# A sparse-attention block on one core: two shared PSUM banks, a new order of its stages, and shorter square roots

## The chip, the core and the metric

The kernel runs on one core of one Trainium2 chip. Its engines are TensorE (PE, with its weight loads PEld), VectorE (DVE), ScalarE (ACT), GpSimd (POOL) and SyncE (SP), which issues the DMAs. Each takes its own instructions in the order in which they stand in the program, and they meet at semaphores. The metric is device time in microseconds, less is better.

## The reference, cut to what matters

The input is x of shape [16, 512, 128]: 16 batches of 512 tokens.

```
...
q, k, v = heads(x @ w_q.T), heads(x @ w_k.T), heads(x @ w_v.T)      # 16 heads of 8
q, k = q * rsqrt(mean(q*q) + 1.19e-7), k * rsqrt(mean(k*k) + 1.19e-7)
s = tanh((q k^T / sqrt(8)) / 50) * 50, causal                       # 512 x 512 per head
x = layernorm(x + (softmax(s) v) @ w_o.T)
w = x @ router_w + router_b;  the 63 tokens of the largest w are selected
h = rmsnorm(x_sel, ln1); q, k = rope(h wq), rope(h wk); v = h wv    # 63 x 63 attention, 16 heads
x1 = x_sel + (softmax(q k^T / sqrt(8) + mask) v) @ wo
x2 = x1 + gelu(rmsnorm(x1, ln2) @ w1) @ w2
x = layernorm(x + (x2 * w at the selected tokens, x elsewhere))
...
```

## The kernel before, in words

The batches go in eight pairs. The dense attention is one batch (`/0` or `/1`) at a time, in eight groups of two heads. For each group PE computes scores in two halves (`scores`, L1116, 3 and 5 matmuls) into `ps_s`, ACT applies tanh to each half (L655) and one exp to the group (L667), POOL zeroes what is not causal (L562, four instructions), and every second group PE multiplies by v (`pv`, L1130, 32 matmuls) into `ps_y`.

Around it stand stages, each cut into uses of PE and steps of DVE:

- `prep` (a batch): transpose x, q, k and v, their norm, and the split of q and k into two f16 parts; the low parts are made by POOL (`prep.lo`, L577).
- `fin` (a batch): normalise y (`yU`, `y0`, `y1`, `yT`), project (`wo`), add x (`res`), layernorm: `fin.ln` (moments, L836 to L844), `fin.root1`, `fin.root2`, `fin.x1` (L863).
- `route` (a batch): w is reduced by DVE (`route.w`, L871) from a product made by POOL (`route.xw`), spread and transposed (`row`), and tokens are ranked with `ge` (L887), `eq` (L894) and `rank`.
- `sel` (a pair): gather, rmsnorm, q, k, v with rope, and `R`: the mask's selected rows (L1220, 16 matmuls).
- `att` (a pair): scores `S0`, `S1`, softmax, `P0`, `P1` (transposes), `PV`, `oT`, `wo`, `x1f`, rmsnorm (`ss`, roots, `hn`), `h2T` (L1297), `w1`, gelu in which POOL makes `hh` and `hu`, and ACT a tanh (`g`).
- `late` (a pair): `w2`, scatter (`sc0`, `sc1`), `z0`, `z1`, layernorm (`late.norm`, L1060), store.

**What sets the order.** The body for pair p is 16 steps of two half-steps. In each PE first issues half of the next group's scores and then what `PE_ORDER` lists; DVE and POOL follow `VE_ORDER` and `POOL_ORDER`. `att.P0@-2` is use P0 of stage att for pair p-2, `prep.qk0/0@1` is for batch 0 of pair p+1. The tables don't say when something runs: an engine goes on to its next entry when that entry's semaphores allow. Pairs 3 to 6 run in a hardware loop, the others are written out. After the last scores three more bodies drain `sel`, `att` and `late`.

**PSUM.** `prep` has bank `ps_a`. All other short uses share bank `ps_m`. A use may be written when the one before it has been read: `BANK_READ` lists, by use, the DVE steps to wait for, as `"sel.R": ["sel.vv1@0"]`.

**Roots.** 1/sqrt is a guess from the bits and three Newton rounds of three instructions: with the variance 11 dependent instructions, in two parts. `a & b` in `VE_ORDER` makes two roots in turn, instruction by instruction; six of the seven roots of a pair of batches are made so (`fin/1 & att`, `prep/0 & sel`, `fin/0 & late`), and `prep/1` stands alone.

```
def step(make, name, after=None):            # each step waits for the one before it in its stage
    ...
for step, name, buf, *_ in problems:         # problems: one or two roots
    step(lambda: nc.vector.tensor_tensor(buf[:, 2], buf[:, 1], buf[:, 1], ALU.mult), f"{name}_a{i}")
for step, name, buf, *_ in problems:
    step(lambda: nc.vector.scalar_tensor_tensor(buf[:, 2], buf[:, 2], -0.5, buf[:, 0], ALU.mult, ALU.mult), f"{name}_b{i}")
for step, name, buf, *_ in problems:
    step(lambda: nc.vector.scalar_tensor_tensor(buf[:, 1], buf[:, 2], 1.5, buf[:, 1], ALU.add, ALU.mult), f"{name}_c{i}")
```

## Time and profile before

| | |
|---|---|
| median of 3 runs | 953.69 us (952.84 to 954.15) |
| the profiled execution | 953.16 us, span of its instructions 951.4 us |
| busy: PE, DVE, ACT, POOL | 731.0, 678.2, 609.6, 407.3 us |
| chain that ended last, shares | PE 46%, DVE 29%, issue 13%, ACT 7%, POOL 2% |
| granted TensorE clock, mean | 0.795 of full |

A row of the page names the line, the engine, the operation, output and inputs, a count, the busy time with the mean of one, and the idle time of the engine in front of it with what ended it. A wait row names the waiting engine and line, and whom it waited for. The chain of waits follows the execution back from its end. "issue" is time for which the profile shows no reason. Times in a timeline count from the span's start.

### The profile page before, as it was taken

Reading aid. Unit: us, or ns where it says so; the run is one execution under the profiler, and the core shown is the slowest. Engines: PE = TensorE matmul, PEld = TensorE weight load, DVE = VectorE, ACT = ScalarE, POOL = GpSimd, SP = SyncE. Lnnn points to the kernel's source line nnn. Section 1 sums busy time; section 2 is a strip of 40 time slices with the busy share of each in tenths; the row PEclk is TensorE's granted clock in tenths of the full one; section 3 lists DMA queues with packets and bytes.
Section 4 is the critical chain, followed back from the end, with each engine's and each line's share of the span. In section 5 each row is a group of like instructions: output and inputs, shape, how many; then the busy total and the mean of one; then the engine's idle time right before and its main releaser. Section 6 shows DMA issues by size and latency. Waiting matters only on the chain.

```text
span 951.4 us, 15701 instructions
## 1 busy us (share of the span) xinstructions
PE 731.0 (77%) x4976; PEld 398.3 (42%) x4976; DVE 678.2 (71%) x2013; ACT 609.6 (64%) x403; POOL 407.3 (43%) x776
## 2 busy tenths in 40 slices
...
DMA packets 96898, 36.40 MB, mean 38 GB/s; under 512 B 68018, under 2 KB 94146, under 8 KB 96834
## 3 DMA queue, kind: packets, MB, share of 16 engines
q1 hardware_dynamic: 96834, 35.67, 16.2%
q8 instruction: 25, 0.41, 0.2%
q14 instruction: 39, 0.32, 0.1%
...
## 4 chain that ended last, share of the span: by engine, by line
PE 46%; DVE 29%; issue 13%; ACT 7%; POOL 2%; DVEq 1%; DMA 1%; POOLq 0%; SPq 0%; ACTq 0%
PE ps_y L1130 10%; PE ps_s L1116 9%; PE ps_m L1220 5%; ACT pr L667 4%; PE ps_m L1137 4%; DVE junk L887 3%; ACT th L655 2%; PE ps_a L1168 2%; PE ps_a L1161 2%; PE ps_m L1319 2%; PE ps_m L1187 2%; PE ps_m L1205 2%; PE ps_m L1266 2%; PE ps_m L1280 2%; PE ps_m L1303 1%
## 5 line engine op out<-in xcount | busy, mean ns | idle before, releaser
L655 ACT ACTIVATE th<-ps_s 128x1024 f32<-128x1024 f32 (+1 forms) x256 | 308.8, 1236 | 155.3 <-PE ps_s L1116 149.8
L667 ACT ACTIVATE pr<-th 128x2560 f32<-128x2560 f32 x128 | 298.8, 2335 | 31.0 <-PE ps_y L1130 31.0
L1116 PE MATMUL ps_s<-q_st,k_st 32*128 32x128 f16 (+3 forms) x1024 | 209.8, 342 | 26.2 <-ACT th L655 22.0
L562 POOL TENSOR_SCALAR_AFFINE_SELECT pr<-pr 128x256 f32<-128x256 f32 (+2 forms) x512 | 194.7, 413 | 0.0
L1130 PE MATMUL ps_y<-pr,v_aug 128*32 128x512 f32 (+3 forms) x2048 | 178.2, 496 | 3.8 <-POOL pr L562 3.8
L1116 PEld LDWEIGHTS ps_s<-q_st,k_st 32*128 32x128 f16 x1024 | 84.6, 102 | 125.0 <-issue 60.5
L577 POOL TENSOR_TENSOR st<-qk,st 128x1024 f16<-128x1024 f32 x32 | 73.1, 2303 | 103.7 <-DVE st L803 103.7
L1130 PEld LDWEIGHTS ps_y<-pr,v_aug 128*32 128x32 f32 x2048 | 65.3, 121 | 114.2 <-issue 96.2
L620 POOL TENSOR_TENSOR pool_mark<-head_of 128x1 f32<-128x1 f32 x128 | 26.5, 207 | 187.5 <-ACT pr L667 187.3
L565 POOL TENSOR_TENSOR st<-qk 128x1024 f32<-128x1024 f32 x16 | 30.3, 1893 | 48.9 <-DVE qk L776 48.9
L887 DVE TENSOR_SCALAR_CACHE_REDUCE junk<-w_wide,x 128x512 f32<-128x512 f32 x64 | 47.7, 746 | 2.0
L1220 PE MATMUL ps_m<-masks,E 128*64 128x512 f32 x128 | 43.0, 834 | 7.6 <-DVE vv L960 7.6
L1161 PE MATMUL ps_a<-wT,xT 128*128 128x256 f32 x128 | 41.8, 455 | 8.9 <-DVE qk L776 7.9
L565 POOL TENSOR_TENSOR r<-x,rw_row 128x512 f32<-128x512 f32 x16 | 18.9, 1178 | 58.6 <-DVE x L863 58.6
L1297 PE MATMUL ps_m<-ident,hn 128*128 128x128 f32 x8 | 3.8, 472 | 51.3 <-DVE hn L1017 51.3
L641 ACT ACTIVATE hq<-hu 128x512 f32<-128x512 f32 x8 | 5.0, 630 | 56.9 <-POOL hu L565 56.9
L813 DVE COPY y_u<-ps_y 128x512 f32<-128x512 f32 x32 | 21.9, 684 | 25.3 <-PE ps_y L1130 25.2
L565 POOL TENSOR_TENSOR k_wide<-qkT,head_of 128x1024 f32<-128x1024 f32 x16 | 30.1, 1904 | 19.0 <-DVE qkT L966 19.0
L894 DVE SCALAR_TENSOR_TENSOR junk<-w_wide,x,later 128x512 f32<-128x512 f32 (+1 forms) x64 | 36.0, 562 | 2.0
L637 ACT ACTIVATE pm<-pm 128x1008 f32<-128x1008 f32 x8 | 8.4, 1044 | 42.3 <-DVE pm L979 42.3
L776 DVE COPY qk<-ps_a 128x512 f32<-128x512 f32 x32 | 22.0, 686 | 18.1 <-PE ps_a L1161 18.1
L882 DVE COPY w_wide<-ps_m 128x512 f32<-128x512 f32 x16 | 11.1, 691 | 32.1 <-PE ps_m L1137 24.7
...
## 6 DMA issues: line engine op xcount, KB each, us to landing
...
q_st<-st SPq DMA_TRANSPOSE x16, 4.5
k_st<-st SPq DMA_TRANSPOSE x16, 4.8
...
```

The costliest lines, as they stand in the source:

```text
L562: return nc.gpsimd.affine_select(out=buf, in_=buf, compare_op=ALU.is_ge, fill=0.0, base=0, pattern=[[0, n], [1, P]] if n > 1 else [[1, P]] ...
L565: mul = lambda out, a, b: nc.gpsimd.tensor_tensor(out, a, b, ALU.mult)
L577: pl["prep"].done(nc.gpsimd.tensor_tensor(lo_parts[s], qk_twice[s], hi_parts[s], ALU.subtract), f"lo_{part}", b)
L655: nc.scalar.activation(th[:, gi % 2, c0:c1], ps_s[:, c0:c1], ACT.Tanh, scale=1.0 / (QK_SCALE ** 2 * DH ** 0.5 * SOFTCAP))\
L667: nc.scalar.activation(pr[:, gi % 4, :], th[:, gi % 2, :], ACT.Exp, scale=SOFTCAP)\
L887: step(lambda: nc.vector.tensor_scalar(junk[:, :], w_wide[:, :], x1[:, k, c, D:D + 1], 0.0, ALU.is_ge, ALU.add, accum_out=cnt_ge[:, c:c + ...
L894: step(lambda: nc.vector.scalar_tensor_tensor(junk[:, 0:n], w_wide[:, P * c:], x1[:, k, c, D:D + 1], later[:, 0:n], ALU.is_equal, ALU.mult ...
L1116: last = mm(ps_s[:, c:c + S - P * kb], k_st[32 * j:32 * j + 32, k, kb, g, :], q_st[32 * j:32 * j + 32, k, kb:NT, g, :], start=True, stop=True)
L1130: last = mm(ps_y[32 * j:32 * j + 32, P * kb:S], v_aug[:, k, kb, h, :], pr[:, gi % 4, c:c + S - P * kb], start=(q % 2 == 0 and kb == 0), st ...
L1137: last = tr(ps_m[:, P * c:P * c + P], src(c), ident[:, :])
L1161: last = mm(ps_a[:, 2 * D * (t % 2):2 * D * (t % 2) + 2 * D], xT[:, P * t:P * t + P], wT[:, 0:2, :].rearrange("p a d -> p (a d)"), start=T ...
L1220: last = mm(ps_m[SLOTS * k:SLOTS * k + SLOTS, :], E[:, c, SLOTS * k:SLOTS * k + SLOTS], masks[:, k, c, :], start=(c == 0), stop=(c == NT - 1))
```

## The change

**Banks.** The table `BANK` gives every short use one of the two banks, "a" or "m", `prep` among them, so that a use and the next mostly lie in different banks; `BANK_READ` is new with it. The setup's three matmuls go to `ps_y`.

**Order.** `PE_ORDER`, `VE_ORDER` and `POOL_ORDER` are new; ACT's is as it was.

**Roots.** A polynomial of four instructions takes the place of the three rounds: guess, a, t, then u2, u3, u4, y. The variance is folded into the moments or the reduction in front, but for `prep`, which keeps its own. Eight instructions for `prep`, seven for the others, each root by itself. The moments lose one instruction of six (`sum`), and now four of the five are chained.

```diff
-                for i in (0,) if first else (1, 2):
-                    for step, name, buf, *_ in problems:
-                        step(lambda: nc.vector.tensor_tensor(buf[:, 2], buf[:, 1], buf[:, 1], ALU.mult), f"{name}_a{i}")
...
+                    step(lambda: nc.vector.tensor_scalar(y.bitcast(I32), w.bitcast(I32), -0.5, RSQRT_GUESS, ALU.mult,
+                                                         ALU.add), f"{name}_guess")
+                    step(lambda: nc.vector.tensor_tensor(t, y, y, ALU.mult), f"{name}_a")
+                    step(lambda: nc.vector.tensor_tensor(w, t, w, ALU.mult), f"{name}_t")
+                else:
+                    step(lambda: nc.vector.scalar_tensor_tensor(t, w, q3, w, ALU.add, ALU.mult), f"{name}_u2")
+                    step(lambda: nc.vector.scalar_tensor_tensor(t, t, q2, w, ALU.add, ALU.mult), f"{name}_u3")
+                    step(lambda: nc.vector.scalar_tensor_tensor(t, t, q1, w, ALU.add, ALU.mult), f"{name}_u4")
+                    step(lambda: nc.vector.scalar_tensor_tensor(y, t, q0, y, ALU.add, ALU.mult), f"{name}_y")
...
+BANK = {
...
+    "sel.R": "m",
...
+    "sel.qkv": "a",
+}
...
-    "sel.R": ["sel.vv1@0"],
+    "sel.R": ["prep.xT/1@2", "sel.hnT@0"],
...
-                bank_free("att.h2T", q)
-                pe["att"].done(tr(ps_m[:, 0:P], hn[:, :], ident[:, :]), "h2T", q)
+                bank_free("att.h2T", q)
+                pe["att"].done(tr(at("att.h2T")[:, 0:P], hn[:, :], ident[:, :]), "h2T", q)
...
-                tr(ps_m[:, 0:P], rw_wide, ident[:, :])
+                tr(ps_y[:, 0:P], rw_wide, ident[:, :])
...
+                if q == 0 and isinstance(b.no, int) and b.no == 0:
+                    t_.wait_ge(setup_ve, SETUP_ROUTER)
```

**Place 1: PE, from the projection `wo` of `att` to `h2T`** (the transpose of `hn`), in pair 2's body. Before:

```order
L1292 MATMUL ps_m<-wo,oT 128x128
L1116 MATMUL ps_s<-q_st,k_st 128x256 x2
L1116 MATMUL ps_s<-q_st,k_st 128x384
L1116 MATMUL ps_s<-q_st,k_st 128x128
L1116 MATMUL ps_s<-q_st,k_st 128x512
L1297 MATMUL ps_m<-ident,hn 128x128
```

The change, from right behind `wo`:

```order
L1156 MATMUL ps_s<-q_st,k_st 128x384
L1156 MATMUL ps_s<-q_st,k_st 128x128
L1156 MATMUL ps_s<-q_st,k_st 128x512
L1196 MATMUL ps_m<-ident,x_in 128x128 x4
L1156 MATMUL ps_s<-q_st,k_st 128x256 x2
L1156 MATMUL ps_s<-q_st,k_st 128x384
L1156 MATMUL ps_s<-q_st,k_st 128x128
L1156 MATMUL ps_s<-q_st,k_st 128x512
L1156 MATMUL ps_s<-q_st,k_st 128x384
L1156 MATMUL ps_s<-q_st,k_st 128x128
L1156 MATMUL ps_s<-q_st,k_st 128x512
L1339 MATMUL ps_a<-ident,hn 128x128
```

Between `wo` and `h2T` stand now three halves of scores and the transpose `prep.xT` instead of one half of scores, and `h2T` goes to `ps_a`. Behind `h2T` comes `pv` and then `w1`; before it was `w1` and then `pv`.

**Place 2: DVE, the start of the body.** `cnt_eq` is `eq`, `den` is the softmax's sum, `k_wide<-ps` is a copy of `P0` or `P1`, `qk<-ps` copies q and k. Before:

```order
L894 SCALAR_TENSOR_TENSOR junk,cnt_eq<-w_wide,x,later 128x512
L894 SCALAR_TENSOR_TENSOR junk,cnt_eq<-w_wide,x,later 128x384
L894 SCALAR_TENSOR_TENSOR junk,cnt_eq<-w_wide,x,later 128x256
L894 SCALAR_TENSOR_TENSOR junk,cnt_eq<-w_wide,x,later 128x128
L776 COPY qk<-ps_a 128x2x2x128
L986 TENSOR_REDUCE den<-pm 128x16
L987 RECIPROCAL rden<-den 128x16
L991 COPY k_wide<-ps_m 128x512
L900 TENSOR_TENSOR rank<-cnt_ge,cnt_eq 128x4
L903 TENSOR_SCALAR coef<-cnt_ge 128x4
L907 TENSOR_TENSOR E<-rank,slot_no 128x4x64
L776 COPY qk<-ps_a 128x2x2x128
```

The change:

```order
L923 TENSOR_SCALAR junk,cnt_ge<-w_wide,x 128x512 x4
L810 COPY qk<-ps_a 128x2x2x128
L810 COPY qk<-ps_m 128x2x2x128
L847 COPY y_u<-ps_y 128x512
L1023 TENSOR_REDUCE den<-pm 128x16
L1024 RECIPROCAL rden<-den 128x16
L822 COPY v_aug<-ps_m 128x16x2x8 x2
L854 RECIPROCAL rd<-ps_a 128x32
L856 TENSOR_TENSOR y_tm<-ps_a,rd 128x4x64
L1028 COPY k_wide<-ps_m 128x512
L826 TENSOR_REDUCE qn_v<-st 128x128
L1028 COPY k_wide<-ps_a 128x512
```

The second copy of q and k, for which PE's `prep.v` waits, stands behind one copy and not behind `eq`, `den`, `P0`'s copy and `rank`, which come later; the two copies read different banks.

**Place 3: DVE, from `hn` of `att` to `route.w`** (the reduction of `r`, L871 before and L907 now). Before:

```order
L1017 TENSOR_SCALAR hn<-x1f,sel_v 128x128
L863 TENSOR_SCALAR x<-r,mv,ln_v 128x128 x4
L1020 TENSOR_SCALAR h2T<-ps_m,g 128x128
L1060 TENSOR_SCALAR y_out<-y_out,mv,lo_v 128x128 x8
L1026 COPY hb<-ps_m 128x512
L871 TENSOR_REDUCE x<-r 128x4
```

The change:

```order
L1055 TENSOR_SCALAR hn<-x1f,sel_v 128x128
L783 TENSOR_SCALAR ln_v<-ln_v 128x4
L785 TENSOR_TENSOR ln_v<-ln_v 128x4
L786 TENSOR_TENSOR ln_v<-ln_v 128x4
L788 SCALAR_TENSOR_TENSOR ln_v<-ln_v 128x4
L789 SCALAR_TENSOR_TENSOR ln_v<-ln_v 128x4
L790 SCALAR_TENSOR_TENSOR ln_v<-ln_v 128x4
L791 SCALAR_TENSOR_TENSOR ln_v<-ln_v 128x4
L1058 TENSOR_SCALAR h2T<-ps_a,g 128x128
L899 TENSOR_SCALAR x<-r,mv,ln_v 128x128 x4
L907 TENSOR_REDUCE x<-r 128x4
```

Before, `h2T`, the eight instructions of `late.norm` and a copy stood between `fin.x1` (`x<-r,mv`) and `route.w`, which waits for POOL's product of x1. Now `route.w` stands right behind `fin.x1`, and `late.norm` is behind `g`, ahead of `late.proc`.

## Rows read from the trace of the kernel before

**Rows 1.** The page: busy time of each engine (us, share of the span).

```profile
PE 731.0 (77%) x4976; PEld 398.3 (42%) x4976; DVE 678.2 (71%) x2013; ACT 609.6 (64%) x403; POOL 407.3 (43%) x776
```

**Rows 2.** Windows (us, busy us of PE, PEld, DVE, ACT, POOL, clock): middle, one pair, last pair, tail.

```profile
193.75:713.50 519.75, 435.29 (x3106) 236.90 (x3107) 410.79 (x1208) 378.95 (x251) 249.62 (x470) 0.82 0.18 41
501.90:607.65 105.75, 88.03 (x621) 47.97 (x622) 83.79 (x249) 75.78 (x51) 49.87 (x94) 0.81 0.16 35
713.50:810.60 97.10, 82.12 (x603) 44.12 (x605) 73.37 (x231) 74.72 (x50) 43.23 (x91) 0.83 0.12 27
810.60:951.40 140.80, 77.50 (x395) 48.54 (x395) 81.02 (x294) 18.54 (x13) 23.18 (x32) 0.60 0.04 12
```

**Rows 3.** Waits, 501.9 to 607.65 us (total us, times, longest us).

```profile
ACT th L655 <- PE ps_s L1116: 25.2, 13, 3.9
...
PEld ps_m L1297 <- DVE hn L1017: 8.1, 1, 8.1
...
PEld ps_m L1220 <- DVE vv L960: 3.3, 2, 1.6
...
PEld ps_a L1161 <- DVE qk L776: 2.6, 2, 2.0
```

**Rows 4.** Timeline of DVE, 553 to 563.5 us (start us, duration us).

```profile
554.84 2.09 DVE L841 TENSOR_TENSOR mv<-stats 128x4 f32<-128x4 f32 x1
...
557.30 0.29 DVE L1009 TENSOR_TENSOR x1f<-xs,ps_m 128x128 f32<-128x128 f32 x1
...
562.18 0.40 DVE L1017 TENSOR_SCALAR hn<-x1f,sel_v 128x128 f32<-128x128 f32 x1
```

**Rows 5.** Groups on POOL, 501.9 to 607.65 us (busy us, mean ns, idle before).

```profile
L562 POOL TENSOR_SCALAR_AFFINE_SELECT pr<-pr 128x128 f32<-128x128 f32 (+1 forms) x64 | 24.5, 414 | 0.0
L577 POOL TENSOR_TENSOR st<-qk,st 128x1024 f16<-128x1024 f32 x4 | 9.2, 2317 | 15.9 <-DVE st L803 15.9
...
L565 POOL TENSOR_TENSOR r<-x,rw_row 128x512 f32<-128x512 f32 x2 | 2.4, 1176 | 5.1 <-DVE x L863 5.1
```

**Rows 6.** Timeline of DVE: steps of two roots in turn, and of `prep/1`'s alone.

```profile
504.50 0.17 DVE L750 TENSOR_TENSOR ln_v<-ln_v 128x4 f32<-128x4 f32 x1
...
504.71 0.16 DVE L752 SCALAR_TENSOR_TENSOR ln_v<-ln_v 128x4 f32<-128x4 f32 x1
...
547.20 0.29 DVE L750 TENSOR_TENSOR qn_v<-qn_v 128x128 f32<-128x128 f32 x1
547.52 0.29 DVE L752 SCALAR_TENSOR_TENSOR qn_v<-qn_v 128x128 f32<-128x128 f32 x1
```

**Rows 7.** Chain of waits near the end (start us, us): one root alone, first and last step.

```profile
922.61 0.17 DVE sel_v L744
...
924.53 0.17 DVE sel_v L755
```

**Rows 8.** Group on DVE, 501.9 to 607.65 us: `eq`, both batches (busy us, mean ns).

```profile
L894 DVE SCALAR_TENSOR_TENSOR junk<-w_wide,x,later 128x512 f32<-128x512 f32 (+3 forms) x8 | 4.5, 560 | 0.2
```

**Rows 9.** Chain of waits, 812 to 895 us.

```profile
836.33 1.13 DVE den L986
...
858.77 2.88 DVE y_out L1060 x8
...
878.50 1.95 PE ps_m L1205 x8
...
890.47 0.42 DVE hb L951
...
892.21 2.82 PE ps_m L1220 x5
```

**Rows 10.** Timeline of PE, 903 to 920 us.

```profile
903.24 1.97 PE L1266 MATMUL ps_m<-k_wide,qkT 128*64 128x512 f32 x4 [1.27 <-POOL k_wide L565]
906.09 1.98 PE L1266 MATMUL ps_m<-k_wide,qkT 128*64 128x512 f32 x4 [0.89 <-DVE sc L972]
...
913.77 1.09 PE L1137 MATMUL ps_m<-ident,pm 128*128 128x128 f32 x4 [1.30 <-DVE k_wide L991]
```

More of the change, by code:

```diff
@@ L93 @@
 PE_ORDER = (
-    ["prep.qk0/1@0", "route.wrow/0@-1"], ["pv.2/1@-1"],
-    ["pv.3/1@-1", "att.P0@-2"], ["prep.qk1/1@0"],
-    ["att.P1@-2", "prep.v/1@0"], ["fin.y1T/1@-1"],
-    ["fin.yT/1@-1"], ["fin.wo/1@-1", "pv.0/0@0"],
-    ["att.PV@-2", "prep.xT/0@1"], [],
-    ["att.oT@-2", "att.wo@-2"], ["att.h2T@-2"],
-    [], ["att.w1@-2", "pv.1/0@0"],
-    ["route.wrow/1@-1"], ["prep.qk0/0@1", "fin.y0T/0@0", "pv.2/0@0"],
-    ["prep.qk1/0@1"], ["late.w2@-2"],
-    ["late.sc0@-2", "pv.3/0@0", "prep.v/0@1", "late.sc1@-2"], ["sel.gather@-1"],
@@ new lines @@
+    ["prep.xT/0@1"], [],
+    ["att.h2T@-2"], ["pv.1/0@0", "att.w1@-2"],
+    ["route.wrow/1@-1"], ["prep.qk0/0@1", "pv.2/0@0"],
+    [], ["prep.qk1/0@1", "fin.y0T/0@0", "late.w2@-2"],
+    ["pv.3/0@0", "prep.v/0@1"], ["late.sc0@-2"],
+    ["late.sc1@-2", "fin.y1T/0@0"], ["sel.gather@-1", "fin.yT/0@0"],
+    [], ["fin.wo/0@0", "sel.ET@-1", "pv.0/1@0"],
+    ["sel.hnT@-1"], ["prep.xT/1@1", "sel.qkv@-1"],
+    ["sel.R@-1"], ["sel.qkT@-1", "pv.1/1@0", "sel.RT@-1"],
+    [], ["sel.msel@-1", "fin.y0T/1@0"],
@@ L121 @@
-    ["att.hn@-2", "fin.x1/1@-1", "att.h2T@-2", "late.norm@-3"],
-    ["att.h@-2"],
-    ["route.w/1@-1", "route.row/1@-1", "fin.yU0/0@0", "att.hp@-2", "route.ge/1@-1", "prep.qk0/0@1", "fin.y0/0@0",
-     "att.g@-2"],
-    ["late.proc@-2", "route.eq/1@-1"],
-    ["prep.qk1/0@1"], ["late.z0@-2"],
-    ["fin.yU1/0@0", "route.rank/1@-1"], ["late.z1@-2", "prep.v/0@1", "prep.ss/0@1", "sel.xs@-1"],
-    ["sel.ss@-1"], ["fin.y1/0@0", "prep.root1/0@1 & sel.root1@-1", "fin.yT/0@0"],
-    ["prep.root2/0@1 & sel.root2@-1", "sel.hn@-1"], ["sel.ET@-1", "prep.qkn/0@1", "sel.hnT@-1", "prep.hi/0@1"],
```

396 lines of the change are left out of this document (218 added, 178 removed).

## The prediction

> **What bounds the kernel now.** I began with the totals on the page. PE is busy 77% of the span, DVE 71% and ACT 64% [rows 1]: no engine is full, so the time lies in how they wait for each other. The windows cut the span into stages that are told apart by PE's wait for `R`: from 193.75 to 713.5 us five pairs of batches take 519.75 us, one of them 105.75; a last pair with scores takes 97.1; then there is a tail of 140.8 us in which ACT has 18.5 us of work [rows 2]. In one pair PE is busy 88.0 of 105.75 us, DVE 83.8 and ACT 75.8. ACT stands still 25.2 us in that pair for scores that PE hands over late [rows 3], so ACT sets nothing. PE and DVE each have some 20 us of idle time, and the chain of waits changes between these two all the time. Two engines that work in order and wait for each other's next piece bound the pair; neither's sum does.
>
> The head, up to 193.75 us, I leave as it is: the table's stages are few there and ACT runs almost without gaps.
>
> **The roots, in the middle: nothing.** Per pair they shrink from 7 x 11 = 77 instructions to 2 x 8 + 5 x 7 = 51, and the moments lose one of six three times: 29 fewer. But what costs is the step. Two roots in turn go at 0.21 us for two steps (504.50 to 504.71), a root of `prep` alone at 0.32 [rows 6], another root alone at 0.19 a step (922.61 to 924.53, ten steps) [rows 7]. `prep/1` alone: three steps less, -1.0 us. `fin/1 & att` and `fin/0 & late`: 11 x 0.21 = 2.3 before, 2 x 7 x 0.19 = 2.7 now, +0.4 each. `prep/0 & sel`, where the small steps hid in the long ones: 11 x 0.32 = 3.5 before, 8 x 0.32 + 7 x 0.19 = 3.9 now, +0.4. Moments: -0.1 x 3. The sum is -0.1 us per pair: what the polynomial saves, the lost partner takes.
>
> The Trainium skill (VectorE: DVE Perf Modes, "Rules for kernel authors") says of chained DVE instructions that their number is to be made small, since each pays its flush. By it the 29 instructions would each be worth a step, and the pair would get some 4 us of DVE back. The rows of the roots in turn don't agree: in turn, a step costs half.
>
> **The order and the banks, in the middle: -9.0 us per pair taken away.**
> - PE's longest wait is 8.1 us for `hn` in front of `h2T` [rows 3]. DVE reads `wo`'s result at 557.30 and ends `hn` at 562.58, 5.3 us [rows 4]. Now only `ss`, `res`, one root, the moments of `fin` and `hn` itself stand in that stretch: 0.6 + 0.6 + 7 x 0.19 + 1.5 + 0.3 = 4.3, so -1.0. In front of `x1f` stood `xT` and `fin.ln`, in which one instruction took 2.09 us [rows 4]; with half of `xT` and the short steps I put at 3.4 us what they kept `x1f` waiting; now it is `rank`, 0.9: -2.5. PE meanwhile has two more halves of scores and a transpose (place 1), 1.9 us by what they take in this pair. Of 8.1 us 2.7 are left: **-5.4**.
> - `R` waited for DVE's last read of q, k, v from its bank (`vv`): 3.3 us in two waits, the longer 1.6, one of them in this pair and the other at its edge [rows 3]. It is in the other bank now and needs `hnT` alone: **-1.6**.
> - `prep.qk1` waited up to 2.0 us for the copy of `qk0` out of its bank [rows 3], and the copy came behind `eq` (place 2). Now the banks differ and the copies come first: **-2.0**.
>
> **What comes in their place: +3.4 us.** `route.w` stands right behind `fin.x1`, and between them POOL has a product to make, 1.18 us [rows 5], with two hand-overs 1.5. Behind it on DVE wait `late.root2`, `yU0`, `h`, `row`, and PE's `wrow` and `w1`'s successor for them. `hp` stands only one copy behind `h`, and needs `hh` of POOL: +0.7. Each of the two can meet POOL's four instructions for a group, 4 x 0.41 = 1.7 [rows 5], which I count every second time for one: +0.9. Small hand-overs for `ss` behind `sq`: +0.3. Net -5.6 us a pair, and it counts in the five pairs of the middle and in the last: 6 x 5.6 = **34 us**.
>
> How much of a removed wait comes through is not shown by this trace. Below: nothing, if the next wait is as late. Above: all 9.0, and 10 with the small bank hand-overs; ACT's 75.8 us a pair would still not be reached. I take the net value, since both directions of waits are counted in it.
>
> **The tail, -12.5 us.** Here the chain is almost unbroken and each piece counts.
> - `den` starts at 836.33, behind `row`, `ge` and `eq` [rows 9]. `eq`, 2.2 us a batch [rows 8], goes behind, and a 0.6 us copy comes in front: 1.6 us earlier. `late.norm`, 2.88 us on the chain (858.77), moves under PE's `w2`: -1.4 after the new wait for POOL. Uses P0, P1 and `fin`'s four no longer take turns with one bank: -1. The gather (878.50) comes **4.0** earlier.
> - `R` starts at 892.21, q, k, v were there at 890.47 [rows 9]: **-1.8**. Half a late root, six steps, no longer stands between R's copy and qkT: **-1.1**.
> - S1 starts at 906.09, 0.9 after S0 is done [rows 10]: **-0.7**. P1 starts at 913.77 behind P0's copy [rows 10]; in the other bank it follows P0, and `PV` comes **1.8** earlier. `sc1` behind `sc0` the same way: **-0.8**.
> - Three roots on the chain with no partner (`sel`, `att`, `late`), four steps of 0.19 less each [rows 7]: **-2.3**.
>
> **Sum.** 34 + 12.5 = 46.5. The profiled execution took 953.16 us, 1.8 more than its span; 953.2 - 46.5 = 906.7. It lies 0.5 below the median of the runs, so I forecast **907 us**, 890 to 922 if it goes this way. A difference below 0.2%, 2 us, can't be told from none.
>
> **Rivals.**
> 1. *All of it comes through, and PE gets its clock.* PE's granted clock is 0.82 in the middle and 0.60 in the tail, where PE has gaps [rows 2]. With 10 us a pair and the tail: 953 - 60 - 12.5 = 881; 876 to 890. For it: nothing else in the pair is full. Against: DVE's 83.8 us stay, and three new waits for POOL. The Trainium skill (TensorE: Matmul & The Clock Gate, "HAM oscillation — how this bites in real kernels") says that gaps of PE throttle it and steady work doesn't, which would speak for this case; the two clocks in the rows agree.
> 2. *The middle stays.* The waits just move: PE waits less at `h2T` and more at `w1` or `wrow`, because DVE stands at `route.w`. 9 us away, 9 back: 953.7 - 12.5 = 941; 922 to 951. For it: the pair is a cycle of two engines with 16 or so changes, and only three were looked at.
> 3. *Slower, by POOL in DVE's way.* DVE's instructions with both inputs in SBUF stand still while POOL works: one took 2.09 us instead of 0.15 [rows 4], and there is a 4.6 us pair of L577 [rows 5] right behind `prep.hi` in the new order too, now with `rank`, `ss`, a root and the moments after it. Three DVE steps (`route.w`, `hp`, `ss` of `prep`) wait closely for POOL; each can cost 1.2 + 1.7 + 0.3 = 3.2, 9.6 in all, and the blocked steps 4.6 + 2.0 more: +16.2 against -9.0, 6 x 7.2 - 12.5 = +31, 985 us. It decides from 9.0 + 12.5 / 6 = 11 us a pair on; just past it the time is 955 to 965. The Trainium skill (SBUF — State Buffer, "Who interferes with whom") says that a DVE instruction with two SBUF inputs and a POOL instruction that reads SBUF block each other for the whole instruction. By it the change has fewer such instructions (6 a root instead of 9), yet more of them beside L577. The 2.09 us row agrees.
> 4. *The change does nothing that counts*: within 2 us, if 2 and 3 cancel.
>
> **How the numbers follow.** Forecast (890 to 922) 0.47, rival 1 0.18, rival 2 0.20, rival 3 0.12, rival 4 0.03. Faster by over 0.2%: 0.47 + 0.18 + 0.20 = 0.85; within 0.2%: 0.03; slower: 0.12. The range reaches from rival 1's 876 to 948 near the upper end of rival 2; left out are rivals 3 and 4 (0.15) and 0.05 at both ends.
>
> **What would show it.** In the changed profile: PE's wait for `hn` at `h2T` under 3.5 us a pair; `R`'s wait for `vv` gone; the pair in the middle at 99 to 101 us; DVE's busy time a pair within 2 us of 83.8 though 29 instructions fewer; new idle time of DVE in front of the reduction in `route.w`, about 1.5 us, and in front of `hp`; from the last `R` but one to the end 128 us instead of 140.8. I am wrong if the pair keeps its 105.75 us, if DVE's busy time falls by 4 us a pair (then the partner was worth nothing), or if its waits for POOL pass 11 us.

## The result and the profile after

The changed kernel takes 903.5 us in the median of four runs (899.54 to 906.80); the kernel before, run beside it, takes 953.92. The ratio is 0.9468, with an interval of 0.9428 to 0.9509: faster by 5.3%. 907.0 us were forecast. The profiled execution took 903.66 us, its span 901.9 us. In this document a median takes in all runs of a kernel, while a ratio leaves out the slow ones, those over 1.5% above its fastest, so that the two can differ.

From the page of the kernel after: the span, the totals, the granted clock in 40 slices (tenths), the shares of the chain, and the group of ACT's tanh.

```profile
span 901.9 us, 15411 instructions
...
PE 720.7 (80%) x4976; PEld 401.4 (45%) x4976; DVE 664.5 (74%) x1781; ACT 608.8 (68%) x403; POOL 410.3 (45%) x776
...
PEclk9558886788699979796799968996779878975655
...
PE 42%; DVE 31%; issue 14%; ACT 8%; POOL 3%; DVEq 1%; DMA 0%; POOLq 0%; SPq 0%; ACTq 0%
...
L691 ACT ACTIVATE th<-ps_s 128x1024 f32<-128x1024 f32 (+1 forms) x256 | 307.6, 1236 | 133.1 <-PE ps_s L1156 127.7
```

Against [rows 1] DVE has 232 instructions and 13.7 us less, PE 10.3 us less on the same 4976 matmuls. ACT's wait for scores falls from the 149.8 us on the page of before to 127.7. The chain is still PE's and DVE's. The clock changes all the time, and its mean is 0.792 (before 0.795).

PE's first matmul of `R` (L1262, before L1220) again cuts the program. Windows of the kernel after: the five pairs of the middle, two of these pairs by themselves, the last pair, the drain (columns as in [rows 2]).

```profile
188.73:686.57 497.84, 431.00 (x3106) 240.67 (x3106) 402.68 (x1068) 378.94 (x251) 251.23 (x471) 0.84 0.19 42
482.72:581.61 98.89, 84.30 (x621) 46.72 (x621) 81.42 (x220) 75.71 (x51) 49.91 (x95) 0.86 0.17 38
581.61:686.57 104.96, 91.66 (x622) 52.16 (x622) 81.50 (x220) 75.73 (x51) 49.85 (x95) 0.79 0.15 33
686.57:778.00 91.43, 78.67 (x599) 41.58 (x599) 74.37 (x211) 74.50 (x51) 46.74 (x93) 0.87 0.17 35
778.00:901.90 123.90, 70.78 (x393) 46.33 (x392) 80.04 (x258) 16.88 (x12) 23.42 (x32) 0.62 0.05 13
```

| stretch, us | before | after | forecast |
|---|---|---|---|
| head, up to `R` of the first pair | 193.8 | 188.7 | 193.8 |
| six pairs | 616.8 | 589.3 | 582.8 |
| drain | 140.8 | 123.9 | 128.3 |
| span | 951.4 | 901.9 | 904.9 |

In the six pairs PE's idle time goes from 99.4 to 79.6 us and its busy time from 517.4 to 509.7, over all six `R`-to-`R` windows of each trace. So 19.8 of the 27.5 us are waits, and 7.7 us are PE's own busy time on the same matmuls, with a higher granted clock (mean 0.82 in [rows 2], now 0.84 over the first five). The two pairs shown have the same instructions and much the same waits, and yet take 98.9 and 105.0 us: PE is busy 84.3 us at clock 0.86 in one and 91.7 at 0.79 in the other. The clock has a part of its own.

Waits in the pair from 482.72 us (total us, times, longest us), of which the first two stand where [rows 3] had ACT's 25.2 and `h2T`'s 8.1 (L783, the step right behind `hn`, is named for `hn`, which `h2T` reads):

```profile
ACT th L691 <- PE ps_s L1156: 19.2, 8, 4.1
...
PEld ps_a L1339 <- DVE ln_v L783: 3.3, 1, 3.3
...
PEld ps_m L1196 <- DVE x1f L1046: 2.6, 1, 2.6
...
PE ps_a L1179 <- DVE y_u L847: 2.3, 1, 2.3
...
PEld ps_m L1262 <- DVE xT L805: 1.3, 1, 1.3
DVE x L907 <- POOL r L601: 1.3, 1, 1.3
```

A row with `PEld` tells the wait of the weight load, a row with PE that of the matmul itself. `h2T` waits 3.3 us and no longer 8.1. But a new wait of 2.6 stands just ahead of it, at `prep.xT` (L1196) for `x1f`; `R` waits for `prep.xT`'s copy instead of `vv`; `y1T` waits 2.3 for `y_u`; and `route.w` waits 1.3 for POOL.

Where the wait for `x1f` comes from shows in the timelines of that pair (start us, duration us): DVE, then POOL, then PE, whose idle time stands in brackets.

```profile
531.30 0.29 DVE L1041 COPY oT<-ps_m 128x128 f32<-128x128 f32 x1
531.51 1.76 DVE L936 TENSOR_TENSOR rank<-cnt_ge,cnt_eq 128x4 f32<-128x4 f32 x1
533.31 2.06 DVE L939 TENSOR_SCALAR coef<-cnt_ge 128x4 f32<-128x4 f32 x1
535.40 0.42 DVE L943 TENSOR_TENSOR E<-rank,slot_no 128x256 f32<-128x256 f32 x1
535.75 0.28 DVE L1046 TENSOR_TENSOR x1f<-xs,ps_m 128x128 f32<-128x128 f32 x1
536.06 0.42 DVE L1050 CUSTOM_DVE_ANT_0 hn<-x1f 128x128 f32<-128x128 f32 x1
...
540.19 0.29 DVE L1055 TENSOR_SCALAR hn<-x1f,sel_v 128x128 f32<-128x128 f32 x1
```

```profile
530.76 4.59 POOL L613 TENSOR_TENSOR st<-qk,st 128x1024 f16<-128x1024 f32 x2 [12.99 <-DVE st L837]
```

```profile
532.87 0.39 PE L1334 MATMUL ps_m<-wo,oT 128*128 128x128 f32 x2
533.19 0.60 PE L1156 MATMUL ps_s<-q_st,k_st 32*128 32x384 f16 x3
536.08 0.65 PE L1196 MATMUL ps_m<-ident,x_in 128*128 128x128 f32 x4 [2.29 <-DVE x1f L1046]
...
540.61 0.47 PE L1339 MATMUL ps_a<-ident,hn 128*128 128x128 f32 x1 [2.77 <-DVE ln_v L783]
```

PE is through with `wo` (L1334) at 533.26. DVE is at `rank` and `coef`, two steps on 4 elements a partition, which take 1.76 and 2.06 us instead of about 0.16, since POOL's L613 runs until 535.35; they end when its two instructions end. `x1f` begins at 535.75. In [rows 4] it was a step of the moments that stood still there for 2.09. The new order has only put other steps in POOL's way. The Trainium skill (SBUF — State Buffer, "Who interferes with whom") gives both kinds: two inputs from SBUF, as `rank` has, or the fast two-port mode, which a `tensor_scalar` like `coef` can take. By that rule the copies from PSUM around them run on. The trace agrees: `oT`'s copy took its 0.29 us.

### The profile page after: what moved, and what is told of

Same layout as the page of the kernel before. It is cut to its first block, busy times and chain, and to the rows that moved or that the text cites. A ratio compares the mean times of both kernels' runs of the same rounds, so it can differ in the third digit from the quotient of the medians.

```text
span 901.9 us, 15411 instructions
## 1 busy us (share of the span) xinstructions
PE 720.7 (80%) x4976; PEld 401.4 (45%) x4976; DVE 664.5 (74%) x1781; ACT 608.8 (68%) x403; POOL 410.3 (45%) x776
## 4 chain that ended last, share of the span: by engine, by line
PE 42%; DVE 31%; issue 14%; ACT 8%; POOL 3%; DVEq 1%; DMA 0%; POOLq 0%; SPq 0%; ACTq 0%
PE ps_y L1172 12%; PE ps_s L1156 9%; ACT pr L703 4%; ACT th L691 4%; PE ps_a L1322 3%; PE ps_a L1179 2%; DVE stats L870 2%; PE ps_m L1179 2%; PE ps_a L1247 2%; DVE qk L831 2%; PE ps_a L1203 2%; DVE junk L930 2%; PE ps_m L1203 1%; PE ps_m L1308 1%; PE ps_m L1262 1%
## 5 line engine op out<-in xcount | busy, mean ns | idle before, releaser
L691 ACT ACTIVATE th<-ps_s 128x1024 f32<-128x1024 f32 (+1 forms) x256 | 307.6, 1236 | 133.1 <-PE ps_s L1156 127.7
L1156 PE MATMUL ps_s<-q_st,k_st 32*128 32x256 f16 (+3 forms) x1024 | 198.6, 331 | 27.4 <-ACT th L691 23.4
L598 POOL TENSOR_SCALAR_AFFINE_SELECT pr<-pr 128x256 f32<-128x256 f32 (+2 forms) x512 | 197.7, 420 | 0.0
L1172 PE MATMUL ps_y<-pr,v_aug 128*32 128x512 f32 (+3 forms) x2048 | 194.0, 531 | 0.2 <-POOL pr L598 0.2
L1156 PEld LDWEIGHTS ps_s<-q_st,k_st 32*128 32x128 f16 x1024 | 82.6, 100 | 122.7 <-issue 44.9
L1172 PEld LDWEIGHTS ps_y<-pr,v_aug 128*32 128x32 f32 x2048 | 68.9, 128 | 128.3 <-issue 118.5
L613 POOL TENSOR_TENSOR st<-qk,st 128x1024 f16<-128x1024 f32 x32 | 73.3, 2311 | 104.4 <-DVE st L837 104.4
L1262 PE MATMUL ps_m<-masks,E 128*64 128x512 f32 x128 | 30.2, 615 | 5.7 <-DVE xT L805 5.7
L601 POOL TENSOR_TENSOR z_base<-x,coef 128x512 f32<-128x512 f32 x16 | 16.6, 1054 | 39.3 <-DVE y_out L1087 38.9
L1322 PE MATMUL ps_a<-vv,k_wide 128*128 128x32 f32 x128 | 28.0, 393 | 2.1 <-DVE k_wide L1028 2.1
L1322 PEld LDWEIGHTS ps_a<-vv,k_wide 128*128 128x128 f32 x128 | 27.0, 321 | 5.3 <-DVE k_wide L1028 2.9
L1179 PE MATMUL ps_a<-ident,y_u 128*128 128x128 f32 x96 | 17.0, 305 | 11.4 <-DVE y_u L847 11.4
```

The costliest lines, as they stand in the source:

```text
L598: return nc.gpsimd.affine_select(out=buf, in_=buf, compare_op=ALU.is_ge, fill=0.0, base=0, pattern=[[0, n], [1, P]] if n > 1 else [[1, P]] ...
L601: mul = lambda out, a, b: nc.gpsimd.tensor_tensor(out, a, b, ALU.mult)
L613: pl["prep"].done(nc.gpsimd.tensor_tensor(lo_parts[s], qk_twice[s], hi_parts[s], ALU.subtract), f"lo_{part}", b)
L691: nc.scalar.activation(th[:, gi % 2, c0:c1], ps_s[:, c0:c1], ACT.Tanh, scale=1.0 / (QK_SCALE ** 2 * DH ** 0.5 * SOFTCAP))\
L1156: last = mm(ps_s[:, c:c + S - P * kb], k_st[32 * j:32 * j + 32, k, kb, g, :], q_st[32 * j:32 * j + 32, k, kb:NT, g, :], start=True, stop=True)
L1172: last = mm(ps_y[32 * j:32 * j + 32, P * kb:S], v_aug[:, k, kb, h, :], pr[:, gi % 4, c:c + S - P * kb], start=(q % 2 == 0 and kb == 0), st ...
```

## Experiments

The first group takes the change apart: order, banks and roots.

**1. Banks alone.** Before's tables, its roots merged; each short use in one of two banks, in turn by PE's order.

```diff
+BANK = {
+    "prep.qk0/1": "a",
+    "route.wrow/0": "m",
+    "att.P0": "a",
+    "prep.qk1/1": "m",
...
+}
```

> The kernel before, with its order and its roots, but each short use in one of the two banks, in turn by its place in PE's order (with msel in the bank of S0). Theory W (the prediction's: each removed wait comes through): R's wait for vv goes (1.6 us a pair), half of qk1's (1.0), and in the tail R 1.8, P1 and PV 1.8, sc1 0.8, S1 0.7, fin 1.0: 954 - 6 x 2.6 - 6 = 932 us, 926 to 938. Theory C (the middle goes by PE's granted clock, which falls behind its 7.5 us gap in front of h2T): that gap stays as it is, so the middle stays, and only the tail gives its 6 us: 944 to 950 us, with the clock of the middle at 0.81 to 0.82.

982.3 us, ratio 1.0289 (1.0266 to 1.0312). Both theories fail (926 to 938, 944 to 950): it is slower. A pair takes 109.2 us and PE's wait for `hn` is still 7.2 us. `prep` and the rest now wait for each other's reads: the scatter's first half (`sc0`) waits 3.4 us in a pair for the second copy of q and k, which the old DVE order puts behind `eq`.

**2. Order alone.** The changed kernel with the old two banks. That needs two swaps.

```diff
-    [], ["att.PV@-2", "fin.yT/1@-1", "pv.0/0@0"],
-    ["att.oT@-2"], ["fin.wo/1@-1", "att.wo@-2"],
+    [], ["fin.yT/1@-1", "att.PV@-2", "pv.0/0@0"],
+    ["att.oT@-2"], ["att.wo@-2", "fin.wo/1@-1"],
```

> The changed kernel, its order and its roots, but prep's uses in one bank and all others in the other as before; for that two neighbours are swapped on PE (yT/1 ahead of PV, att.wo ahead of fin.wo/1), which else would wait for each other in a circle. Theory W: 903.5 + 6 x 2.6 (R's wait and half of qk1's are back) + 4.5 (P1 and PV, S1, sc1, fin in the tail) = 924 us, 917 to 930. Theory C: what counts is the gap in front of h2T, which the order has cut to some 5 us in two pieces; it stays cut, and the clock with it: 906 to 914 us.

1093.6 us, ratio 1.1439 (1.1381 to 1.1496), 190 us more than with both; the two theories had forecast at most 930. Waits in one of its pairs (699 to 829 us):

```profile
ACT th L691 <- PE ps_s L1156: 52.7, 17, 11.4
...
PEld ps_m L1262 <- DVE vv L997: 14.1, 2, 7.1
```

ACT's 19.2 us for scores are 52.7, and `R` waits up to 7.1 us for `vv`, since it stands right behind the q, k, v whose bank it now shares (of the two waits one is at the pair's edge). This pair takes 129.8 us, 30.9 more than the change's from 482.72 us; PE idles 14.3 us longer and is busy 16.6 us longer, at a clock of 0.71 and not 0.86. My price of 1.6 us for that wait was its length in an order that was made for one bank. The new order leans on the banks; a price list of single waits doesn't see that.

**3. Some banks.** Before's tables; only uses of `sel` and two of `fin` move, where `prep` has nothing in its bank.

```diff
+BANK = {
...
+    "fin.y0T/1": "a",
...
+    "fin.yT/0": "a",
...
+    "sel.gather": "a",
+    "sel.hnT": "a",
...
+    "sel.qkT": "a",
+    "sel.qkv": "a",
+}
```

> The kernel before, its order and its roots; gather, yT/0, hnT, qkv, qkT and y0T/1 move to bank ps_a, where prep has no use at that time, so that the uses of sel take turns between two banks and nothing waits for prep. The prediction's terms: R's wait 1.6 us a pair, R in the tail 1.8: 954 - 9.6 - 1.8 = 942 us, 939 to 947. Theory C: R's wait goes, the gap at h2T and the clock stay: a pair changes by less than 1 us, 950 to 954 us.

946.7 us, ratio 0.9815 (0.9756 to 0.9874). The four runs fall apart: 934.2 and 942.0, which go with theory W (939 to 947) or beyond it, and 951.5 and 952.0, which go with theory C (950 to 954). So the runs don't decide between the two. The profiled run is the one of 951.5 us, and one of its pairs shows why it is near before's:

```profile
600.84:706.72 105.88, 90.94 (x623) 48.40 (x622) 84.77 (x249) 76.24 (x50) 49.81 (x95) 0.77 0.15 33
```

`R`'s wait for `vv` is gone, PE idles 14.9 us where it idled 17.7, and the pair has its 105.9 us as before, because PE is busy 90.9 us at 0.77 instead of 88.0 at 0.81. What the wait gave, the clock took in that run; of the two shorter runs there is no trace.

**4 and 5. Roots alone**, in before's order and banks: each by itself, and two in turn. The first is shown; the second keeps the `&`.

```diff
-    ["sel.qkv@-1", "late.ln@-2"],
-    ["fin.root1/0@0 & late.root1@-2", "sel.R@-1", "fin.root2/0@0 & late.root2@-2"],
+    ["sel.qkv@-1", "late.ln@-2"], ["fin.root1/0@0", "late.root1@-2", "sel.R@-1", "fin.root2/0@0", "late.root2@-2"],
```

> The kernel before, its order and its banks, with the polynomial roots and shorter moments, each root by itself, its first part and then the next root's first part. The prediction's step: -0.1 us a pair, -2.3 in the tail: 951 us, 949 to 954, DVE's busy time a pair within 0.5 us of 83.8. Rival (the partner was worth little, each of the 29 instructions saved counts): DVE's busy time falls by 4 us a pair and the time to 925 to 935 us.

> The same, but two roots made in turn wherever the kernel before did so. The prediction's prices: prep/1 -1.0 us a pair, fin & att and fin & late 4 x 0.21 less each, prep & sel 3 x 0.32 less, moments 0.3: DVE's busy time falls by some 3.9 us a pair against the kernel before and is 3.8 below that of the single roots. In time, if all of it lies on the path: 954 - 24 - 3 = 927; if it mostly lies beside other work 945 to 951. Rival (the partner is worth nothing): the same DVE busy time and the same device time as with single roots, within 2 us.

Single 945.5 us (0.9906, 0.9889 to 0.9923), in turn 938.2 (0.9773, 0.9692 to 0.9854). The first lies between the prediction's span (949 to 954) and the rival's (925 to 935), the second between 927 and the 945 to 951. A pair with single roots:

```profile
608.95:714.75 105.80, 88.34 (x621) 48.07 (x621) 81.31 (x220) 75.77 (x51) 49.71 (x94) 0.81 0.16 33
```

DVE has 2.5 us less than in [rows 2] and the pair is just as long, 105.8 in three pairs one after the other: these pairs don't feel it. This profiled run took 951.3 us at a mean clock of 0.791, the four others 944.7 to 945.6 at 0.803 to 0.804; where they were shorter no trace shows. A partner is worth something: 7.3 us of time by the medians, 12.7 by the ratios, and, over the span, 14 us of DVE (653.0 to 639.0).

**6 and 7. Newton in the new kernel, and the last corner of the square.** The first is the changed kernel, the second before's order and banks with single roots.

```diff
-                    step(lambda: nc.vector.tensor_tensor(w, t, w, ALU.mult), f"{name}_t")
...
+                for i in (0,) if part == 1 else (1, 2):
+                    step(lambda: nc.vector.tensor_tensor(t, y, y, ALU.mult), f"{name}_a{i}")
+                    step(lambda: nc.vector.scalar_tensor_tensor(t, t, -0.5, w, ALU.mult, ALU.mult), f"{name}_b{i}")
+                    step(lambda: nc.vector.scalar_tensor_tensor(y, t, 1.5, y, ALU.add, ALU.mult), f"{name}_c{i}")
```

> The changed kernel with the three Newton rounds again, each root by itself (10 or 11 instructions instead of 7 or 8), the shorter moments kept. The prediction's prices: prep 2 x 3 x 0.32, the five others 3 x 0.19 each, 4.8 us of DVE a pair more; in the tail three roots on the chain, 3 x 3 x 0.19 = +1.7. If the middle hides it: 905 to 908 us. If all of it is on the path: 903.5 + 6 x 4.8 + 1.7 = 934 us. I expect half: 915 to 922, since the root of att is in front of h2T (+0.6 to the gap) and DVE has some 17 us idle a pair.

> The order and the banks of the kernel before, three Newton rounds, each root by itself, the shorter moments: the fourth corner of a square of order and banks against roots. The other three are measured: order before, polynomial 945.5; order and banks of the change, Newton 965.5; both 903.5. Theory T (order and banks are worth their 42 us with either root, and the polynomial its 62 with either order): 1007 us. Theory I (the new order works close to what DVE can do, so that only there DVE's 5.2 us a pair count; the old order waits elsewhere): DVE's busy time 86.5 a pair, and the time 950 to 970 us.

| medians, us | Newton, single | polynomial, single | the polynomial's worth |
|---|---|---|---|
| order and banks of before | 973.7 | 945.5 | 28 |
| order and banks of the change | 965.5 | 903.5 | 62 |
| worth of order and banks | 8 | 42 | |

The ratios are 1.0099 (1.0068 to 1.0130) for the new order and 1.0199 (1.0171 to 1.0228) for the old one with Newton. The first misses its expectation by far: 915 to 922 us were expected, and 934 if every step counted. The additive theory T (1007) falls; 973.7 lies 4 us above theory I's span, so the old order isn't deaf to DVE either. And 973.7 is 19 to 20 us above the kernel before, which differs from it by the partners of its roots and the longer moments: with Newton's chains the partners are worth that much. One pair each, Newton in the new order and then in the old:

```profile
507.07:617.53 110.46, 92.04 (x621) 50.86 (x621) 87.65 (x241) 76.05 (x51) 49.74 (x95) 0.78 0.16 34
```

```profile
512.20:621.52 109.32, 89.45 (x622) 49.13 (x622) 85.48 (x241) 75.66 (x51) 50.88 (x94) 0.80 0.15 34
```

In the new order DVE has 6.2 us more than in the change's pair from 482.72 us (81.4), and the pair is 11.6 longer: PE idles 3.8 us longer, and is busy 7.7 longer, at 0.78 instead of 0.86. That pair is one of the change's shorter ones; over all six pairs, 644.0 us against 589.3, PE idles 19.0 us longer and is busy 35.7 longer. The two pairs shown are nearly alike: with ten or eleven steps a root the new order is worth almost nothing.

**8. Newton in two roots**, those whose `hn` PE waits for, by the same edit for `sel` and `att` alone.

> The changed kernel with Newton rounds in two of the seven roots of a pair, those of sel and att, whose hn PE waits for; 3 x 0.19 us more each, 1.2 us of DVE a pair of the 5.2 that cost 62 us in all seven. Theory A (the amount of DVE work counts, wherever it stands): 903.5 + 62 x 1.2 / 5.2 = 918 us, 912 to 924. Theory P (the place counts: only what stands in front of hn lengthens PE's gaps): most of the 62 us come here, 940 to 965 us.

916.1 us, ratio 0.9595 (0.9551 to 0.9640): 12.6 more than the change. The four runs lie between 909.2 and 930.0, all far below the 940 of theory P: theory A holds, and the place in front of `hn` is not special. By the prices in the expectation, 1.2 and 5.2 us of DVE a pair, a microsecond costs some 10 us here and 12 in the other five roots ((62 - 12.6) / (5.2 - 1.2)); with this spread the two are not told apart.

The second group asks what the clock and POOL do.

**9. PE kept busy in front of `h2T`**, in the kernel before.

```diff
+FILL = 16
...
+                if not isinstance(q, int) or q + 3 < PAIRS:
+                    ve["prep"].wait(t_, Batch(q + 3, 0), "xT")
+                    for _ in range(FILL):
+                        tr(ps_a[:, 0:P], ident[:, :], ident[:, :])
                 ve["att"].wait(t_, q, "hn2")
```

> The kernel before with nothing moved: in front of h2T, PE first makes 16 transposes of the identity into bank ps_a, which is free there, and only then waits for hn. They take 3.4 us at full clock and 6.9 at half, so they lie inside the gap of 7.5 us and no result comes earlier by them. Not so in the drain of the last two pairs, where they are left out. Theory W (the waits alone make the time, the clock is a bystander): 954 us, 952 to 957. Theory C (the middle goes by the granted clock, which stays at half in and behind that gap): the stretch at half clock, 40 us a pair, ends earlier, by 4 to 12 us; a pair gets 2 to 6 us shorter, and the time is 922 to 942 us.

954.1 us, ratio 0.9982 (0.9968 to 0.9997), no gain that counts; 952 to 957 was theory W's. PE's timeline and the window of that pair:

```profile
554.96 3.67 PE L1299 MATMUL ps_a<-ident 128*128 128x128 f32 x16
562.52 0.47 PE L1302 MATMUL ps_m<-ident,hn 128*128 128x128 f32 x1 [3.89 <-DVE hn L1018]
```

```profile
501.70:607.43 105.73, 91.69 (x638) 51.30 (x638) 83.76 (x249) 75.79 (x51) 49.94 (x94) 0.81 0.16 35
```

The 16 transposes took 3.67 us and left 3.89 idle. The pair is 105.73 us and its clock 0.81, as without them. So half of that gap filled does nothing: theory C in this form falls. Whether the 3.89 us that are left would do for a low clock, this run doesn't show.

**10. PE's gaps filled in the drain**, in the changed kernel, by 2 to 16 such transposes in front of 20 uses, and 6 in front of `h2T` in the middle.

```diff
+                if n:
+                    bank_free(use, unit)
+                for _ in range(n):
+                    tr(at(use, unit if isinstance(unit, Batch) else None)[:, 0:P], ident[:, :], ident[:, :])
```

> The changed kernel with transposes of the identity in PE's gaps, into the bank that the next use takes and ahead of its wait for data: 6 in front of h2T in the middle (2.6 us at half clock, its gap is 2.8), and in the drain behind the last scores 2 to 16 in front of 20 uses, 0.21 us each at full clock, some 80% of each gap there. Theory W: the middle stays; in the drain, where PE works at half clock, each transpose takes 0.43 us and those that outlast their gap delay the chain: 903 to 925 us. Theory C: with PE working, the clock in the drain rises from 0.65 and 0.56 towards 1; PE's 71 us of work there fall towards 45, most of it on the chain: 880 to 893 us.

910.1 us (ratio 0.9508, 0.9463 to 0.9552), 6.6 more than without. The drain of the profiled run:

```profile
789.07:916.40 127.33, 89.11 (x548) 63.62 (x547) 79.58 (x258) 17.28 (x13) 23.45 (x32) 0.75 0.05 13
```

The clock does rise, from 0.62 to 0.75, and the drain takes 127.3 us instead of 123.9. What the faster matmuls gave back, the transposes took: in the chain of waits of this drain they stand with some 13 us. This profiled run was the longest of the four, 918.2 us, and most of what it lost lies ahead of the drain: its six pairs take 603.1 us and not 589.3, with the 6 transposes in front of `h2T`. Theory W (903 to 925) holds in time, though its middle didn't stay; theory C (880 to 893) falls.

**11. `rank` behind `hn`** on DVE, in the changed kernel.

```diff
-    ["route.rank/0@-1", "att.x1f@-2", "att.ss@-2", "fin.res/1@-1"],
-    ["att.root1@-2", "fin.ln/1@-1", "att.root2@-2", "att.hn@-2"],
+    ["att.x1f@-2", "att.ss@-2", "fin.res/1@-1"], ["att.root1@-2", "fin.ln/1@-1", "att.root2@-2", "att.hn@-2", "route.rank/0@-1"],
```

> The changed kernel with one entry of DVE's order moved: rank/0 goes from ahead of x1f to behind hn. In the changed kernel its two smallest steps took 1.76 and 2.06 us instead of 0.15, until POOL's two L613 ended, and x1f began at 535.75, 2.5 us after wo was done. Theory S (these two steps stand still for POOL, one that reads PSUM does not): x1f begins 2.0 us earlier, PE's gap in front of xT/0 goes, the two steps take 0.3 us in all, DVE's busy time a pair falls by some 1.5 us; 903.5 - 6 x 2 = 891 us, 884 to 896. Rival (the steps behind them stand still in their place: ss of att reads SBUF too): nothing is won, 901 to 906 us.

914.1 us, ratio 0.9594 (0.9537 to 0.9651): slower than the change by 10.6. DVE and POOL in one of its pairs, and the pair's window:

```profile
539.62 0.29 DVE L1035 COPY oT<-ps_m 128x128 f32<-128x128 f32 x1
540.64 0.29 DVE L1040 TENSOR_TENSOR x1f<-xs,ps_m 128x128 f32<-128x128 f32 x1 [0.73 <-PE ps_m L1328]
540.96 0.77 DVE L1044 CUSTOM_DVE_ANT_0 hn<-x1f 128x128 f32<-128x128 f32 x1
...
542.43 1.30 DVE L779 TENSOR_TENSOR sel_v<-sel_v 128x1 f32<-128x1 f32 x1
...
547.16 0.29 DVE L1049 TENSOR_SCALAR hn<-x1f,sel_v 128x128 f32<-128x128 f32 x1
547.36 0.16 DVE L930 TENSOR_TENSOR rank<-cnt_ge,cnt_eq 128x4 f32<-128x4 f32 x1
547.55 0.17 DVE L933 TENSOR_SCALAR coef<-cnt_ge 128x4 f32<-128x4 f32 x1
```

```profile
539.07 4.65 POOL L607 TENSOR_TENSOR st<-qk,st 128x1024 f16<-128x1024 f32 x2 [13.25 <-DVE st L831]
```

```profile
487.96:593.85 105.89, 90.96 (x621) 50.42 (x621) 81.34 (x220) 76.03 (x51) 49.53 (x95) 0.81 0.16 35
```

The mechanism is as said: `x1f` begins 1.0 us behind `oT`'s copy instead of 4.5, and `rank` and `coef` take 0.16 and 0.17. But `att`'s sum of squares (L1044) takes 0.77 us instead of 0.42, and a step of its root (L779) 1.30, until POOL ends at 543.72, so that `hn` comes only 1.4 us earlier by the same count. And that small gain is turned over by the clock: the pair has PE idle for 14.9 us, with 14.6 in the pair from 482.72 us of the change, and is 7.0 longer, as PE is busy 91.0 us at 0.81 and not 84.3 at 0.86. Over all six pairs PE idles 77.6 us here and 79.6 in the change, and is busy 527.6 us and not 509.7. Both theories (884 to 896, 901 to 906) missed the time.

**12. Partners for four parts of roots**, in the changed kernel.

```diff
-    ["route.rank/0@-1", "att.x1f@-2", "att.ss@-2", "fin.res/1@-1"],
-    ["att.root1@-2", "fin.ln/1@-1", "att.root2@-2", "att.hn@-2"],
-    ["fin.root1/1@-1"],
...
+    ["route.rank/0@-1", "att.x1f@-2", "att.ss@-2", "fin.res/1@-1"], ["att.root1@-2", "fin.ln/1@-1", "att.root2@-2 & fin.root1/1@-1", "att.hn@-2"],
+    [], ["fin.root2/1@-1 & late.root2@-3", "att.h2T@-2", "prep.xT/0@1", "fin.x1/1@-1", "route.w/1@-1", "fin.yU0/0@0", "att.h@-2"],
```

> The changed kernel with its polynomial, its banks and PE's and POOL's orders as they are; on DVE four parts of roots are again made in turn with a part of another root that stood near: att's second part with fin/1's first, fin/1's second with late's second, fin/0's first with late's first, and prep/0's second with sel's first (for which the sum of squares of sel goes right behind the gather's copy). By the single steps (0.19 alone, 0.21 for two in turn) this takes 0.5 + 0.7 + 0.5 + 0.6 = 2.3 us of DVE off a pair. Theory D (in the new order each microsecond of DVE a pair is worth some 10 us of time, as Newton in all roots, 62 for 5.3, and in two, 12.5 for 1.2, cost): 903.5 - 23 = 880 us, 875 to 890. Rival G (the first microseconds are not on the path, or another clock pattern falls on PE, as when rank was moved): 895 to 912 us, DVE's busy time a pair lower by 2 us all the same.

901.7 us in six runs (892.9 to 906.6), ratio 0.9427 (0.9396 to 0.9458); the intervals of this and of the change overlap, so it can't be told from it. A pair:

```profile
484.44:584.69 100.25, 84.19 (x621) 46.75 (x622) 80.81 (x220) 76.11 (x51) 50.48 (x95) 0.86 0.18 37
```

DVE went down by about 1 us (80.8 here, 81.4 in the change; 1.3 a pair over all six), not 2.3, and the 880 us of theory D stayed far away; the time lies in rival G's span. The 10 us of time that a microsecond of DVE cost on the way up are not to be had on the way down.

What the clock does by itself shows in the changed kernel's own trace. Four windows, the same two stretches of two pairs one after the other:

```profile
549.11:561.11 12.00, 11.53 (x107) 6.52 (x106) 10.44 (x26) 11.03 (x9) 8.79 (x18) 1.00 0.07 19
648.00:660.00 12.00, 11.53 (x108) 6.46 (x105) 10.40 (x26) 11.04 (x9) 8.81 (x18) 1.00 0.06 17
561.11:581.11 20.00, 17.51 (x148) 11.82 (x147) 18.93 (x56) 16.42 (x11) 8.14 (x19) 1.00 0.05 15
660.00:680.00 20.00, 19.24 (x99) 14.24 (x101) 13.78 (x42) 12.91 (x8) 5.74 (x14) 0.58 0.05 16
```

In the first stretch both pairs are alike to 0.06 us on each engine, PE is busy 11.5 of 12 us, and the granted clock is at its upper level, 2.4 GHz. Behind it one pair keeps that level, and the other has 0.58, mostly the lower one, 1.2 GHz; the fall stands at 663.3 us. From 646.2 us, where that pair had got the upper level, up to the fall PE had only two waits named, 0.35 us at 655.5 and 0.27 just before the fall, and the pair that kept its clock had 0.35 and 0.28 at the same places. The Trainium skill (TensorE: Matmul & The Clock Gate, "HAM oscillation — how this bites in real kernels") lays such falls on gaps of PE. These rows don't show that here; the long gap of [rows 3] and the thin drain go with a low clock, but this fall follows no gap that the other pair didn't have too.

## Why the prediction was right, and where not

The time came out 3.5 us below the forecast, and its sum was near in the large: 46.5 us forecast, 50.4 measured. That it came so near is in part luck. The six pairs gave 27.5 us and not 34; a head that was to stay gave 5.0, and the drain 4.4 more than its 12.5. And within the pairs the forecast was for waits alone, 5.6 us a pair: PE's idle time fell by 3.3 a pair, and its busy time, of which the sum says nothing, by 1.3. PE's own waits in the pair of [rows 3], and then one of the changed kernel's pair from 482.72 us:

```profile
PE ps_m L1297 <- DVE hn L1017: 7.5, 1, 7.5
...
PE ps_m L1220 <- DVE vv L960: 1.0, 1, 1.0
```

```profile
PE ps_m L1262 <- DVE xT L805: 1.0, 1, 1.0
```

By its steps:

- **`h2T`'s wait, -5.4: right in mechanism, and near in size**, 8.1 to 3.3 us. A step was missed beside it: `rank` in front of `x1f` was priced at 0.9 us and took 4.2 (531.51 to 535.75), with POOL's L613 beside it, and `prep.xT` on PE, in the bank of `wo`, waits for that. Rival 3 had this mechanism, at the right place even ("now with `rank`"), and the sum left it out. Net of the new gap the stretch gave PE 2.4 us (7.5 to 2.8 + 2.3), not 5.4. This is the largest shortfall in the pairs, 3.0 us each.
- **`R`'s wait, -1.6: wrong.** PE's gap in front of `R` is 1.0 us before and after (the 1.6 was the weight load's wait); `vv` was followed by `prep.xT`'s copy, which `BANK_READ` names in the very line that the diff shows. In experiment 3, where nothing comes in its place, the wait went. In the change `vv` is waited for one use later, 1.4 us in front of `qkT`.
- **`qk1`'s wait, -2.0: gone, but 2.3 us stand new** at `y1T` for `y_u`, which I hadn't looked for. Whether the one became the other no run shows. Net of what took its place no step of the three gave its full size, and waits that the sum doesn't price changed too.
- **The costs put in, +3.4: mostly right.** `route.w`'s wait for POOL was to be 1.5 and is 1.3; `hp`'s was to be 0.7 and is 0.2. What POOL's four instructions and `ss` were to cost, 0.9 and 0.3, no row singles out.
- **"The roots, in the middle: nothing": near in the old order.** What the polynomial saves with single roots, 28 us, the lost partners nearly take, 19 to 20 (experiment 7 against the kernel before). The traced pairs stay at 105.8 us, though the median lies 8.5 us below before and not 2.9, and DVE's busy time a pair falls by 2.5 us and not 0.1. **In the new order it isn't settled:** going back to single Newton roots costs 62 us there, more than twice what it costs in the old one, and Newton with partners wasn't run. The step priced the change against the old chain only. The rule that was weighed there, fewer instructions, would have given DVE some 4 us a pair; the trace shows 2.4, between that and the forecast.
- **"The order and the banks": right as one sum, not in parts.** With the new roots they give 42 us, with Newton 8; the banks alone (old roots) cost 28 us, the order alone (new roots) 148 against the old order with the same roots. The forecast 34 + 10.2 of the drain was near the 42, but had no such condition.
- **The drain, -12.5: right in kind, -16.9 measured.** The chain of waits of the kernel after (start us, us, what):

```profile
838.62 1.95 PE ps_a L1247 x8
...
849.06 4.61 PE ps_m L1262 x16
...
859.05 1.99 PE ps_m L1308 x4
...
878.26 0.49 PE ps_a L1339
```

From the last `R` but one the gather comes 60.6 us on, before 67.9: 7.3 instead of 4.0. From there to `R` 3.3 are gained (forecast 1.8 and a root's 0.8), from `R` to S0 1.0 (1.1), from S0 to `den` 0.6 (0.7), from there to `PV` 1.2 (1.8), from `PV` to `h2T` 0.8 (a root's 0.8), and from `w2` to the end 2.6 (1.6). The gather's term was the one mis-sized most.
- **The head, unchanged: wrong by 5.0 us.** The same DVE savings act there, 107.4 us busy up to the first `R` instead of 113.0. The roots alone did not shorten the head (198.1 and 195.6 us in the profiled runs of experiments 4 and 5), nor did the order alone (196.7), while the order with its banks did with Newton's roots too (187.6): it is the two together.
- **DVE's busy time a pair within 2 us of 83.8:** 81.4, a miss by 0.4. I reckoned by steps from start to start, where a partner hides one; the busy time counts each record.
- **Rival 1's clock** is part of it after all, without all waits coming through: 7.7 of 27.5 us in the pairs are PE's busy time.

What stays open is when the clock falls. With PE's idle time within 2 us of each other, two pairs of the changed kernel differ by 7.4 us of PE's busy time, and experiment 11's six pairs by 3 us each from the change's. That is more than most terms of the sum, and I could forecast it in none of the twelve experiments. That DVE's microseconds counted nearly double on the way up (6.2 us of DVE, 11.6 of the pair in experiment 6) goes with a lower clock there, but no run here holds the clock fixed, so that the waits' own share was not shown.
